# Gate values of the recurrent layer on four column tiles and all partitions, with new orders of the stages

## The reference, cut to what matters

```python
x = x + _L0_xattn_ref(_layernorm(x), ctx, ctx, ...)   # 16-head cross attention
x = x + _L0_ffn_ref(_layernorm(x), ...)               # 32 x 4 experts, a group of 32 tokens picks one token per expert
x = x + _L1_xattn_ref(_layernorm(x), ctx, ctx, ...)   # 8 heads, gated (mLSTM), below
x = x + _L1_ffn_ref(_layernorm(x), W1, b1, W2, b2)    # ternary weights, 8-bit activations, GELU, 2048 hidden

def _mlstm_head(q, k, v, ig, fg):                     # per batch and head; q = layernormed x, k = v = ctx
    log_fg = jax.nn.log_sigmoid(fg)
    cs = jnp.concatenate([zeros, jnp.cumsum(log_fg, axis=0)])
    log_D = where(ltr, (cs - cs.T)[1:, 1:], -inf) + ig.T
    max_log_D = jnp.max(log_D, axis=-1, keepdims=True)
    D = jnp.exp(log_D - max_log_D)
    C = (q @ (k.T / sqrt(64))) * D
    normalizer = jnp.maximum(jnp.abs(C.sum(-1, keepdims=True)), jnp.exp(-max_log_D))
    return C / (normalizer + 1e-6) @ v                # then an RMS norm per head
# ig = concat(q, k, v) @ igate_kernel + igate_bias, fg likewise: one value per token and head
```

## Time and profile before

| | us |
|---|---|
| three runs | 2091.83, 2093.80, 2101.06 |
| median | 2093.8 |
| the profiled execution, its own time | 2093.38 |
| its span | 2091.5 |

### The profile page before, as it was taken

The page is one execution under the profiler, slowest core; times in us unless marked ns, Lnnn a source line. Parts: engine busy times, 40 slices in busy tenths (PEclk is TensorE's granted clock), DMA queues, the critical chain, the costliest instruction groups (busy, mean ns, idle before and its releaser), DMA issues. The chain is left out here.

```text
span 2091.5 us, 38545 instructions
## 1 busy us (share of the span) xinstructions
PE 1803.8 (86%) x13826; PEld 1086.7 (52%) x13826; DVE 1359.4 (65%) x2609; ACT 1229.1 (59%) x2361; POOL 604.4 (29%) x1107
## 2 busy tenths in 40 slices
PE   7999999999999999999875876347789898888876
PEld 3666666666666666666543533014545445445543
DVE  2767667676676776766745454225778778787874
ACT  2676666666667666676624554123586676776764
POOL 1332233222322322222200000015445445445540
PEclk9999999999999999999998997577789989999998
DMA  7543535435364353444315579775525526425200
GB/s 230 149 116 82 174 96 146 132 81 178 95 152 142 93 184 98 115 138 106 115 53 160 178 263 413 279 262 169 182 71 177 177 71 193 153 75 172 77 16 26
DMA packets 170811, 302.80 MB, mean 145 GB/s; under 512 B 30208, under 2 KB 77888, under 8 KB 162304
## 3 DMA queue, kind: packets, MB, share of 16 engines
q1 hardware_dynamic: 129136, 214.84, 31.8%
q10 hardware_dynamic: 25104, 51.92, 7.4%
q0 software_dynamic: 16384, 33.59, 6.3%
HBM read 165.80 MB, written 67.34 MB: 111 GB/s over the span
## 5 line engine op out<-in xcount | busy, mean ns | idle before, releaser
L570 DVE TENSOR_REDUCE a_negmax<-a_score 128x1 f32<-128x512 f32 x512 | 347.0, 685 | 111.6 <-PE a_score L709 104.3
L330 POOL DMA_DIRECT2D a_q_stack<-a_q_parts x512 | 251.5, 500 | 530.6 <-DVE a_q_parts L564 258.0
L453 ACT ACTIVATE a_prob<-a_score,a_negmax 128x512 f32<-128x512 f32 x512 | 353.8, 693 | 86.3 <-DVE a_negmax L570 85.4
L709 PE MATMUL a_score<-a_k_stack,a_q_stack 128*128 128x512 f32 x512 | 357.4, 698 | 14.1 <-ACT a_prob L453 12.4
L717 PEld LDWEIGHTS a_turn<-a_ident,a_prob 128*128 128x128 f32 x2048 | 253.5, 141 | 137.0 <-issue 95.4
L717 PE MATMUL a_turn<-a_ident,a_prob 128*128 128x128 f32 x2048 | 309.0, 274 | 3.6 <-ACT a_perm L429 1.9
L338 DVE COPY a_probT<-a_turn 128x512 f32<-128x512 f32 x256 | 176.4, 689 | 201.0 <-PE a_turn L717 200.8
L338 ACT COPY a_probT<-a_turn 128x512 f32<-128x512 f32 x256 | 150.0, 586 | 248.6 <-PE a_turn L717 247.7
L2018 PE MATMUL c_ff<-c_w1T,c_xqT 128*128 128x512 bf16 x512 | 130.3, 408 | 43.4 <-DVE c_hid L1837 27.8
L709 PEld LDWEIGHTS a_score<-a_k_stack,a_q_stack 128*128 128x128 f32 x512 | 97.4, 190 | 130.3 <-issue 80.5
L2034 PE MATMUL c_ff<-c_w2T,c_hqT 128*128 128x512 bf16 x512 | 126.1, 404 | 25.6 <-ACT c_hqT L1634 25.5
(11 more groups left out here) (203 smaller groups left out, 3136.0 us busy)
## 6 DMA issues: line engine op xcount, KB each, us to landing
a_k_stack<-a_k_parts SPq DMA_DIRECT2D x512, 64.0 KB, 2.6
a_q_stack<-a_q_parts POOLq DMA_DIRECT2D x512, 64.0 KB, 2.3
scratch_res<-b_chosen SPq DMA_DIRECT2D x32, 1024.0 KB, 11.2
c_res<-scratch_res SPq DMA_DIRECT2D x32, 1024.0 KB, 7.7
a_weights<-in_ffn_W ACTq DMA_DIRECT2D x16, 1024.0 KB, 4.8
c_negm<-scratch_m SPq DMA_DIRECT2D x64, 256.0 KB, 5.2
a_xs<-in_x ACTq DMA_DIRECT2D x8, 1024.0 KB, 5.7
a_x<-in_x ACTq DMA_DIRECT2D x8, 1024.0 KB, 5.8
```

The costliest lines, as they stand in the source:

```text
L330: eng.dma_start(stack[kind][i * DH0:(i + 1) * DH0, M % 2, g, :].bitcast(F32), parts[kind][g * DH0:(g + 1) * DH0, part, :].bitcast(F32)).th ...
L453: nc.scalar.activation(prob[:, U % 4, :], score.bank(U)[:, :], ACT.Exp, bias=negmax[:, u:u + 1], accum_out=sums[:, head_of(U), tile_of(U): ...
L570: nc.vector.tensor_reduce(negmax[:, U % UNITS:U % UNITS + 1], score.bank(U)[:, :], AX.X, ALU.max, negate=True).then_inc(max_ready, 1)
L709: nc.tensor.matmul(score.bank(U)[:, :], stack["Q"][:, M % 2, g, t * P:(t + 1) * P], stack["K"][:, M % 2, g, :], start=True, stop=True).the ...
```

## The change

It has seven parts.

1. A phase's semaphores are cleared by runs of neighbouring numbers, one instruction each.
2. Attention's biases come as one laid-out tensor in one load; before the loop the order becomes K 0, V 0, V 1, the turns, Q 0, V 2, V 3, K 1, and then the first scores.
3. The experts' SP loads rows before it waits, blocks wait for the zeroing of their own buffer, and b1 is loaded late.
4. The tail's gate kernels (laid out, zero-padded to 32 columns), the biases and b2 are loaded by ACT's queue instead of SP's, in three and one loads.
5. `gates` makes a tile of 128 partitions (4 token blocks x 32 rows, 8 used) x 2 x 128 columns: 64 products with 32 columns of weights and 128 moving columns, the cT half first; only the xT half waits for xT. LOGS and ROWS work on 128 partitions x 128 columns. The running sums begin anew in each block of 128 tokens, and the running maximum is handed from block to block by three operations on one column.
6. Three turns of 128 x 128 replace the 11 small ones. Maxima are stored by 4 DMAs and block factors by 3, where each was 1.
7. The orders of PE, DVE, ACT and POOL are new; SP's is as before. ADDB is still after ROOT 0 and before HROOT on POOL.

The core of the diff:

```diff
-                    for s in self.made:
-                        sp.sem_clear(s)
+                    numbers = sorted(s.num for s in self.made)
+                    first = [n for n in numbers if n - 1 not in numbers]
+                    last = [n for n in numbers if n + 1 not in numbers]
+                    for k, n in zip(first, last):
+                        sp.sem_clear(range(k, n + 1))
...
                 product("K", 0, 0, range(C))
+                pe.wait_ge(w_in["Wv"], 16)
+                for t in range(T // 2):
+                    product("V", 0, t, range(C))
                 for c in range(C):
                     turn_tiles("XT", 0, c)
                 pe.wait_ge(wq_ready, 2)
                 product("Q", 0, 0, range(C))
-                pe.wait_ge(w_in["Wv"], 16)
-                for t in range(T - 1):
+                for t in range(T // 2, T):
                     product("V", 0, t, range(C))
+                pe.wait_ge(w_in["Wk"], 16)
+                product("K", 0, 1, range(C))
                 for U in range(AHEAD):
                     scores(U)
-                product("V", 0, T - 1, range(C))
-                pe.wait_ge(w_in["Wk"], 16)
-                product("K", 0, 1, range(C))
...
-                load_tokens(0, 0)
-                load_tokens(0, 1)
+                load_rows(0, 0)
+                load_rows(0, 1)
+                load_blocks(0, 0)
+                load_blocks(0, 1)
...
-                    sp.dma_start(scratch["m"][m], gate_rows[:, 3, :]).then_inc(m_stored, 16)
+                    for t in range(T):
+                        sp.dma_start(scratch["m"][m][:, cols(t)], gate_rows[t * FG:t * FG + H1, 3, :]).then_inc(m_stored, 16)
...
+                act.dma_start(b2e, A["L0_ffn_b2"].rearrange("e s d -> (e s) d")).then_inc(b2e_in, 16)
+                act.dma_start(gate_kernels, A["gate_kernels"][:, C * 2 * FG:]).then_inc(const_in, 16)
+                act.dma_start(gk[:, :, :, :].rearrange("p c k h -> p (c k h)"), A["gate_kernels"][:, 0:C * 2 * FG]).then_inc(const_in, 16)
+                act.dma_start(gb[:, :], A["gate_biases"]).then_inc(const_in, 16)
...
-                    step(nc.vector.tensor_tensor_scan(row(2), one[0:H1, :].to_broadcast([H1, S]), row(1), 0.0, ALU.mult, ALU.add))
+                    step(nc.vector.tensor_tensor_scan(row(2), one[:, :].to_broadcast([P, P]), row(1), 0.0, ALU.mult, ALU.add))
...
                     step(nc.vector.tensor_tensor_scan(row(3), row(1), row(1), -3e38, ALU.max, ALU.max))
...
+                    ends = slice(P - 1, P)
+                    for c in range(LATER):
+                        here, there = slice(c * FG, (c + 1) * FG), slice((c + 1) * FG, (c + 2) * FG)
+                        step(nc.vector.scalar_tensor_tensor(carry[there, :], row(3)[here, ends], carry[here, :], row(2)[here, ends],
+                                                            ALU.max, ALU.add))
+                    step(nc.vector.tensor_scalar(row(3), row(3), carry[:, :], None, ALU.max))
+                    nc.vector.tensor_scalar(later_rows[:, 0, :], row(1), row(3)[:, ends], None, ALU.subtract)
+                    step(nc.vector.tensor_scalar(later_rows[:, 1, :], row(3), carry[:, :], -1.0, ALU.subtract, ALU.mult))
...
-                    for c in range(C):
-                        nc.tensor.matmul(bank[0:GM, :], gk[:, c, :], xT[:, c, :], start=c == 0, stop=False)
-                    for c in range(C):
-                        last = nc.tensor.matmul(bank[0:GM, :], gkv[:, c, :], cT[:, c, :], start=False, stop=c == C - 1)
+                    for part, src in ((gkv, cT), (gk, xT)):
+                        if src is xT:
+                            pe.wait_ge(xT_ready, (m + 1) * C)
+                        for c in range(C):
+                            for k in range(2):
+                                for t in range(T):
+                                    last = nc.tensor.matmul(bank[t * FG:(t + 1) * FG, k * P:(k + 1) * P], part[:, c, k, :], src[:, c, cols(t)],
+                                                            start=src is cT and c == 0 and k == 0, stop=src is xT and c == C - 1,
+                                                            skip_group_check=True)
```

More of the change, by code:

```diff
@@ L1149, in tail_phase @@
     DVE_ORDER = ((("ADD", 0, 0), ("ADD", 1, 0), ("ADD", 2, 0), ("ADD", 3, 0), ("MOM", 0, 0), ("SHIFT", 0, 0),
-                  ("ROWS", 0, 0), ("COLS", 0, 0), ("PROD", 0, 0), ("ADD", 0, 1), ("STATE", 0, 0),
-                  ("ADD", 1, 1), ("ADD", 2, 1), ("STATE", 1, 0), ("PROD", 1, 0), ("ADD", 3, 1),
-                  ("STATE", 2, 0), ("PROD", 2, 0), ("MOM", 0, 1), ("PROD", 3, 0), ("STATE", 3, 0),
-                  ("SHIFT", 0, 1), ("NORM", 0, 0), ("SCALE", 0, 0), ("X3", 0, 0), ("SHIFT", 1, 0),
@@ L1163, in tail_phase @@
-                 (("TOKENS", 0, -2), ("COLS", 0, -1), ("FINISH", 3, -3), ("STATE", 0, -1), ("PROD", 0, -1),
-                  ("EXPAND", 0, -2), ("EXPAND", 1, -2), ("STATE", 1, -1), ("PROD", 1, -1),
-                  ("HSCALE", 0, -2), ("STATE", 2, -1), ("PROD", 2, -1), ("EXPAND", 2, -2),
-                  ("STATE", 3, -1), ("PROD", 3, -1), ("HSCALE", 1, -2), ("NORM", 0, -1),
-                  ("HSCALE", 2, -2), ("EXPAND", 3, -2), ("SCALE", 0, -1), ("FINISH", 0, -2),
-                  ("X3", 0, -1), ("HSCALE", 3, -2), ("FINISH", 1, -2), ("SHIFT", 1, -1),
+                  ("ROWS", 0, 0), ("COLS", 0, 0), ("STATE", 0, 0), ("PROD", 0, 0), ("ADD", 0, 1),
@@ new lines, in tail_phase @@
+                  ("ADD", 1, 1), ("ADD", 2, 1), ("STATE", 1, 0), ("PROD", 1, 0), ("STATE", 2, 0),
+                  ("ADD", 3, 1), ("MOM", 0, 1)),
+                 (("PROD", 2, -1), ("HSCALE", 1, -2), ("PROD", 3, -1), ("STATE", 3, -1), ("EXPAND", 3, -2),
+                  ("HSCALE", 2, -2), ("NORM", 0, -1), ("FINISH", 0, -2), ("SHIFT", 0, 0),
+                  ("HSCALE", 3, -2), ("SCALE", 0, -1), ("FINISH", 1, -2), ("X3", 0, -1),
+                  ("SHIFT", 1, -1), ("ROWS", 0, 0), ("TOKENS", 0, -1), ("COLS", 0, 0),
+                  ("FINISH", 2, -2), ("FINISH", 3, -2), ("STATE", 0, 0), ("PROD", 0, 0),
+                  ("EXPAND", 0, -1), ("EXPAND", 1, -1), ("ADD", 0, 1), ("ADD", 1, 1),
+                  ("HSCALE", 0, -1), ("ADD", 2, 1), ("EXPAND", 2, -1), ("STATE", 1, 0),
+                  ("PROD", 1, 0), ("STATE", 2, 0), ("ADD", 3, 1), ("MOM", 0, 1)),
```

192 lines of the change are left out of this document (97 added, 95 removed), and 35 rows, old and new, of tables (ACT_ORDER, PE_ORDER).

## The result

| | kernel before | changed kernel |
|---|---|---|
| median, us | 2094.87 (2091.83 to 2101.06) | 2048.28 (2044.19 to 2050.30) |
| profiled execution: span, us | 2091.5 | 2042.5 |
| granted clock over the span | 0.930 | 0.937 |

The ratio is 0.9771 (95% interval 0.9744 to 0.9799): 46.6 us less by the medians, 49.0 by the two spans (the profiled execution of the changed kernel was the fastest of its four). The forecast was 2030, 64.2 us less. The span divides as follows, each stretch read from the timelines of both kernels.

A forecast was written before the change was run, and what follows sets the result against it. No single engine bounds the tail, but a loop over all of them (80.3 us a batch). 5.3 + 13.4 + 2.0 + 3.0 + 9 + 31.5 = 64.2 us off 2093.8 gives 2029.6, said as 2030; range 2006 to 2062.

The forecast's parts named there:

- Start of the kernel: Attention before its steady loop: V 0 and V 1 fill PE's wait ahead of the turns, 5.3 us off.
- Clears: Ends of the three phases: one clear instruction per run of semaphore numbers instead of one per semaphore, 13.4 us off.
- Rival C: Clearing a range takes as long as clearing its members singly: 13.4 us back, 2043; chance 0.10.
- Start of the experts: Experts phase: rows load goes first, zeroed blocks wait for one memset only; 2.0 us off (1 to 3).
- Start of the tail: Tail phase: residual loads no longer stand behind the gate kernels, which go to ACT's queue; 3.0 us off (1 to 5).
- first gate chain: Tail's first batch, PE waiting: G 3.9, LOGS 1.3, ROWS 3.0, LATER and turns 1.2; 9 us off.
- Loop: Tail, MIX 3 to next MIX 3 over all engines: period 76.2 for 80.7, seven times, 31.5 us off (7 to 45).
- rival E: Tiled matmuls no faster, G stays at 7 us or more: 2046; chance 0.02.
- A: Tail: PE's list, not the latency, is the loop; period gains 0 to 1 us, 2058; chance 0.22.
- B: Tail's period falls to 74 us, with fewer PE stalls and granted clock staying at 1.0: 2014; chance 0.15.
- D: Slower: SP's queue bounds the tail, late loads hold up MIX 1 to MIX 3; 2101; chance 0.03.
- Signs: Right: UP 0 40 us after MIX 3, first scores at 42. Wrong: UP 0 to MIX 3 above 39, longer gbc waits.

The follow-up runs named there:

- the long ROWS: Changed kernel with the first scan of ROWS given eight times instead of once, on DVE in each batch; 2065.74 us, ratio 0.9861.
- G twice: Changed kernel with the 64 matmuls of G given twice in each batch, same result; 2075.26 us, ratio 0.9906.

## Why the prediction was right or wrong

The direction and the range held, and so did the loop over all engines; its parts held less well. The centre was 18 us too low: 15.2 us by the steps below, the rest because the profiled execution of the changed kernel was 4.1 us faster than its median. By steps:

- **Start of the kernel (5.3 forecast, -4.5 in the spans). This step failed.** It counted the products and the turns and left out ACT's two loads, which stand in ACT's program behind the copy of V 3 and moved with it ahead of the landing of the query stack. They cost 6.6 us at the first scores and 7.8 once the loop runs. My own rule, that each DMA of a moved step counts, was not applied to them. Up to the first store of permT (270.24 before, 271.89 after) only 1.7 of the 4.5 us are there; the remaining 2.9 came later in attention, whose body (first to last store of permT) took 825.8 to 832.4 us in the twelve profiled executions of this case, so that part can't be told from scatter.
- **Clears (13.4 forecast, 11.9 in the spans, 12.4 undone).** 0.064 us each for 0.07. Rival C is out.
- **Start of the experts (2.0 forecast, about 0.6).** SP's loads were issued earlier as forecast, but the rows of batch 1 now stood ahead of the blocks of batch 0. With that one undone the matmul came 1.9 us earlier: the same mechanism as at the start, the same oversight.
- **Start of the tail (3.0 forecast, 2.7) and first gate chain (9 forecast, 8.4).** G's half behind xT was 1.93 us for 2.2, LOGS 2.5 for 2.2; ROWS up to LATER 3.65 us for 2.9 (the carries are 0.70 of it), the term that was sized too small.
- **Loop (31.5 forecast, 25.6, and 21 to 24 in other executions of the same tail). The two halves came out, their terms only in part.** Both halves of the steady batch came within 1.2 us of the forecast (39.5 and 37.4 for 40 and 36.2), a period of 76 to 77. In the first half, TOKENS behind LN 1 gave 3.4 of the 3.5 us, but only because FINISH 2 moved as well. CH 2 still holds LN 1 up, 1.5 us for 2.1, so this gave 0.6 of the 2 us. The chain of the norms, which was put at nothing net, gave 3.4. TOKENS to UP 0 lost the 1 us that was forecast. That the sum lies near 40 is in part luck. The sum on record has two slips of its own: 3.5 + 2 - 1 leaves 41.1 of the 45.6 us, where it took 40, and its rows gave a period of 80.3, where it charged 80.7. By its own terms it would have been 3.0 us a batch or 21 in all. It also charged the same to all seven periods. From square to square they were 77.0, 82.3, 80.4, 80.3, 79.9, 86.8, 70.8 before and 75.1, 76.9, 76.0, 76.9, 76.6, 77.3, 72.2 after. The first gives 1.9, the four steady ones 5.4 to 3.3, the odd one of before 9.5, and the last loses 1.4. I put the gain down to the gates and the shift of UP 3 and SC 1 without asking what each does alone; the runs show that the orders without the short gates lose 13 us, and that in the steady periods the gates without the orders give 0.6 us each.
- **After the loop (nothing forecast besides the clears, 4.3).** The orders' part, 4.1 to 7.0 us in the two pairs of runs, which was put at nothing.
- **G's form.** The forecast took 34 ns a record from the value product; it is 30, so rival E is out. The Trainium skill ("TensorE: Matmul & The Clock Gate", section on 56 against 53.3 ns), by whose slower figure of about 62 ns G would not have gained, isn't borne out for this form. The page gives that figure for hardware decode switched off, and no run here shows which way it was set.
- **Rivals A, B, D.** The period of 76 to 77 is neither A's 80 nor B's 74; the granted clock in the steady batch is 0.96, between the 0.92 of before and B's 1.0. That the new loop runs over the gate chain and isn't PE's list alone is shown by the long ROWS, which adds no work to PE, and by the place where G twice comes out (ahead of LN 1). D's waits exist (35.1 us on POOL for 18.3, 24.9 on DVE for 2.4), so one of the forecast's signs of being wrong came true; the other, more than 39 us from UP 0 to MIX 3, didn't (37.4). What these waits cost inside the loop isn't shown.
- **Signs.** The UP 0 start, TOKENS behind LN 1 and G's rate came as forecast or better. The first scores didn't (47.2 for 42), nor did the gap after the last store: 3.1 us with the 1.7 of the store in it, so 1.4 where less than 1 was forecast.

My sum with the measured terms is -4.5 + 11.9 + 0.6 + 2.7 + 8.4 + 25.6 + 4.3 = 49.0 us, the difference of the spans.

## What to carry to other kernels

When a step moves on an engine's list, look at what its successors on the other engines issue as soon as it is done: here a copy that ended 9 us earlier released 2 MB of loads nobody was waiting for, ahead of 1 MB of small copies that everybody was waiting for. Issue loads with a far due time behind the first use of those with a near one; the fix was three lines moved and cost nothing. And a new order and a shorter step can need each other: measure them in a two by two table before you credit either, and read it by stages of a steady period, not by the total alone. Before you name what an instruction waits for, look at the item right ahead of it in its engine's list.
